# Set-up chains, an output bias on GpSimd and layer 3's first graph ahead of layer 2's tail, in a four-layer graph kernel

## The reference

```python
x = _layernorm(x + _L0_gnn_ref(x, ...))   # relational: sum_r (adj==r) @ ((xW + b_r) * sigmoid(xWWg + bg_r)), relu
x = _layernorm(x + _L1_gnn_ref(x, ...))   # bilinear attention with leaky relu, masked softmax, elu
x = _layernorm(x + _L2_gnn_ref(x, ...))   # 8-head attention, masked; out @ Wo.T + bo
x = _layernorm(x + _L3_gnn_ref(x, ...))   # 8-head additive attention, leaky relu, masked softmax
```

## Time and profile before

| | us |
|---|---|
| median of 3 runs | 737.16 |
| lowest, highest | 736.97, 738.91 |
| profiled execution | 739.22 |
| its span, first to last instruction | 737.5 |

### The profile page before, as it was taken

One profiled execution on the slowest core, in us unless ns is written; L12 is line 12 of the kernel. 1 busy time (PEld: TensorE's weight loads), 2 busy tenths in 40 slices (PEclk: granted clock), 3 DMA queues, 4 the chain that ended last, 5 costly groups with the idle time before them and its releaser, 6 DMA issues.

```text
span 737.5 us, 17528 instructions
## 1 busy us (share of the span) xinstructions
PE 661.7 (90%) x6402; PEld 496.5 (67%) x6402; DVE 604.1 (82%) x1534; ACT 541.3 (73%) x855; POOL 492.8 (67%) x522
## 2 busy tenths in 40 slices
PE   2999799999779999999999998789999999999982
PEld 1788578777446666666666666567777777777751
DVE  4699849999678888888888885789888888888882
ACT  1545379988458777777777776478898998989982
POOL 6377528999675466676566664347777667776685
PEclk9999799999689999999999999899999999999997
DMA  8900000000000000000000000000000000000001
GB/s 232 285 6 1 1 1 1 2 1 2 0 1 2 1 1 2 3 2 2 2 1 3 2 1 1 1 2 2 16 16 30 16 16 16 16 21 26 16 15 44
DMA packets 28885, 14.91 MB, mean 20 GB/s; under 512 B 1920, under 2 KB 28800, under 8 KB 28800
## 3 DMA queue, kind: packets, MB, share of 16 engines
q1 hardware_dynamic: 25344, 12.59, 6.1%
q10 hardware_dynamic: 3456, 1.20, 0.8%
HBM read 9.59 MB, written 4.19 MB: 19 GB/s over the span
## 4 chain that ended last, share of the span: by engine, by line
PE 45%; POOL 19%; DVE 14%; issue 11%; POOLq 7%; ACT 3%; DVEq 0%; ACTq 0%
PE pair L1036 15%; POOL arena L648 7%; POOLq L527 7%; POOL X L532 6%; PE pair L1220 5%; PE quad L1169 4%; DVE arena L1014 3%; DVE nmx L1020 3%; POOL yb L655 3%; PE quad L1084 2%; PE pair L1199 2%; PE pair L1185 2%; PE pair L1191 2%; PE pair L1156 2%; POOL ln L526 2%
## 5 line engine op out<-in xcount | busy, mean ns | idle before, releaser
L634 POOL TENSOR_TENSOR arena<-arena,nmx 128x1024 f32<-128x1024 f32 x64 | 121.3, 1895 | 91.5 <-DVE nmx L965 89.8
L648 POOL TENSOR_TENSOR arena<-arena,nmx 128x1024 f32<-128x1024 f32 x64 | 121.4, 1897 | 78.5 <-DVE nmx L1020 78.4
L1036 PE MATMUL pair<-identf,arena 128*128 128x128 f32 x1088 | 151.0, 281 | 0.9 <-DVE yb L988 0.9
L1036 PEld LDWEIGHTS pair<-identf,arena 128*128 128x128 f32 x1088 | 117.1, 141 | 31.5 <-issue 31.5
L532 POOL TENSOR_SCALAR X<-yb,ln 128x128 f32<-128x128 f32 x256 | 113.2, 454 | 9.0 <-issue 9.0
L526 POOL TENSOR_TENSOR ln<-ln,neghalf 128x4 f32<-128x4 f32 x64 | 66.6, 1041 | 33.0 <-DVE ln L566 32.9
L839 ACT ACTIVATE arena<-quad 128x1024 f32<-128x1024 f32 x64 | 66.0, 1032 | 24.1 <-PE quad L1120 24.0
L956 DVE TENSOR_TENSOR arena<-quad,mask 128x1024 f32<-128x1024 f32 x64 | 77.7, 1214 | 4.8 <-PE quad L1169 4.1
L965 DVE TENSOR_REDUCE nmx<-arena 128x8 f32<-128x1024 f32 x64 | 78.0, 1218 | 1.8
L1020 DVE TENSOR_REDUCE nmx<-arena 128x8 f32<-128x1024 f32 x64 | 78.0, 1218 | 1.7
L1014 DVE TENSOR_TENSOR arena<-quad,arena 128x1024 f32<-128x1024 f32 x64 | 77.7, 1215 | 0.0
(11 more groups left out here) (195 smaller groups left out, 1435.8 us busy)
## 6 DMA issues: line engine op xcount, KB each, us to landing
X<-in_x SPq DMA_DIRECT2D x16, 256.0 KB, 6.1
arena<-in_adj SPq DMA_DIRECT2D x16, 256.0 KB, 6.2
out<-X SPq DMA_DIRECT2D x16, 256.0 KB, 2.3
...
```

The lines of the kernel that those rows point to most:

```text
L634: nc.gpsimd.tensor_tensor(v3(P2[t % 3], HEADS), v3(P2[t % 3], HEADS), nmx2[t % 2][:].unsqueeze(2).broadcast_to([128, HEADS, N]), ALU.add)\
L648: nc.gpsimd.tensor_tensor(v3(p, HEADS), v3(p, HEADS), nmx2[(t - 1) % 2][:].unsqueeze(2).broadcast_to([128, HEADS, N]), ALU.add)\
L1036: last = nc.tensor.transpose(dst[:, cols(i)], src[:, cols(i)], identf[:])
```

## The change

- Set-up: ScalarE issues the two weights, then six DMAs of one row each straight to the partitions 0, 32 and 64 of `bias_rest`, and a dummy Sigmoid. It copies the first three preparations in place of VectorE, which clears `bias3` and splits the bias when the six rows are there; the last subtraction is gone, two copies become one, and the `vx` tiles are cleared afterwards. TensorE starts its preparations with the two weights. GpSimd makes the identity before the other tiles. The copies of the bias to 128 partitions become the last two of the other parameters.
- Layer 0: ScalarE's Relu comes before the `xT` copy. At batch 15 VectorE takes the largest relation behind its masks and makes the flag after `yb` of batch 14. TensorE transposes it, does 13 preparations (in the banks 1, 2, 6, 7) and reads the flag before its last product. The other preparations go into the general branch.
- The output bias is no longer split, and its product leaves `project_out`. GpSimd adds `bo2` to `X` at the third graph of each batch in layer 2, after that batch's transposes. The bias sum and layer 3's weights move into the second step of layer 1 (`late_weights`).
- Layer 3: ScalarE's scaled copy and VectorE's two maxima of graph 0 (`EARLY` = 1) stand at the start of `layer2(64)`.

The diff, cut to its core. Left out are the reordering of the preparation list, the new arguments of the general branches, the bodies of `leaky` and `row_max` (the old lines with t in place of t - 1), and the two additional parameter loads.

```diff
-LAP = 6
+LAP, EARLY = 6, 1
...
+bvo_at = add(bvo[:], qk_bias[:, 3:4].broadcast_to([128, 128]), oT_w[:], oT_at)
+add(wa1[:], w1T[:], a_cols[:, 0:1].broadcast_to([128, 128]), w1_at)
+usual = len(prep)
 gT_at = {k: add(gT[k][:], nat[f"L0_gnn_Wg_{k}"]) for k in ("fwd", "bwd")}
...
+def read_flag(eng):
     eng.wait_ge(sem("flag_set"), 1)
-    value = eng.value_load(flag[0:1, 0:1], min_val=0, max_val=1)
+    return eng.value_load(flag[0:1, 0:1], min_val=0, max_val=1)
+def if_general(eng, value, body):
...
+def masks_of_heads(dve):
...
+def late_weights(dve):
     dve.wait_ge(sem("prep"), bvo_at + 1)
     nc.vector.tensor_tensor(bo2[:], bvo[:], bo_row[:], ALU.add).then_inc(sem("bo_set"), 1)
-    for part in range(3):
-        at = slice(32 * part, 32 * part + 1)
-        dve.wait_ge(sem("bo_set"), 2 + 2 * part)
-        nc.vector.tensor_copy(bo_part[:], bo2[:]).then_inc(sem("bo_set"), 1)
-        dve.wait_ge(sem("bo_set"), 3 + 2 * part)
-        nc.vector.tensor_copy(v3(bo3[at, :], G), bo_part[at, :].unsqueeze(1).broadcast_to([1, G, D]))
-        nc.vector.tensor_tensor(bo2[:], bo2[:], bo_part[:], ALU.subtract).then_inc(sem("bo_set"), 1)
...
+    nc.gpsimd.memset(bias_rest[:], 0.0)
     nc.gpsimd.memset(minus_one[:], -1.0)
-    nc.gpsimd.memset(center[:], 0.0)
-    nc.gpsimd.memset(sel1[:], 0.0)
-    nc.gpsimd.memset(sel2[:], 0.0)
-    nc.gpsimd.memset(headmask[:], 1.0)
-    nc.gpsimd.memset(neghalf[:], -0.5).then_inc(sem("pool_set"), 1)
+    nc.gpsimd.memset(identf[:], 0.0).then_inc(sem("pool_set"), 1)
...
     select(identf[:], [[-1, 128]], 0)
+    nc.gpsimd.memset(ones[:], 1.0)
     nc.gpsimd.tensor_copy(identb[:], identf[:]).then_inc(sem("ident"), 1)
+    nc.gpsimd.memset(neghalf[:], -0.5)
+    for s in range(2):
+        nc.gpsimd.memset(v3(y2x[s][:], G)[:, :, D:D + 1], 1.0)
+    nc.gpsimd.memset(center[:], 0.0)
+    nc.gpsimd.memset(headmask[:], 1.0)
+    nc.gpsimd.memset(sel1[:], 0.0)
+    nc.gpsimd.memset(sel2[:], 0.0).then_inc(sem("pool_set"), 1)
+    steps += 1
+    pool.wait_ge(sem("pool_set"), steps)
...
+    def layer0(b, s, turn):
+        if b == BATCHES - 1:
+            value.append(read_flag(pool))
+        norm_pool(pool, 0, b, s, turn)
+    value = []
+    every_batch(pool, layer0)
+    general_pool(pool, value[0])
...
+        b, j = t // G, t % G
+        if j == 2 and real(b):
+            if b == 0:
+                pool.wait_ge(sem("bo_set"), 1)
+            pool.wait_ge(sem("L2_xT_mm"), b + 1)
+            x = v3(x_of(b), G)
+            nc.gpsimd.tensor_tensor(x, x, bo2[:].unsqueeze(1).broadcast_to([128, G, D]), ALU.add)\
+              .then_inc(sem("L2_x_bo"), 1)
...
+    act.dma_start(nat["L0_gnn_W_loop"], t["L0_gnn_W_loop"][:, :]).then_inc(sem("L0_params"), 16)
+    act.dma_start(nat["L0_gnn_Wg_loop"], t["L0_gnn_Wg_loop"][:, :]).then_inc(sem("L0_params"), 16)
+    act.wait_ge(sem("pool_set"), 1)
+    for part in range(3):
+        at = slice(32 * part, 32 * part + 1)
+        for half, n in enumerate(("b_loop", "bg_loop")):
+            act.dma_start(bias_rest[at, cols(half)], t[f"L0_gnn_{n}"][:, :]).then_inc(sem("bias_loaded"), 16)
+    nc.scalar.activation(act_warm[:], minus_one[:], ACT.Sigmoid)
...
-    act.wait_ge(sem("pool_set"), 1)
+    prep_copies(act, nc.scalar.copy, range(first))
     def layer0(b, s, turn):
+        if real(b):
+            act.wait_ge(sem(f"adj_loaded{b}"), 16)
+            need(act, sem("L0_top"), b - 1)
+            nc.scalar.activation(elu[s][:], adj_of(b), ACT.Relu, bias=minus_one[:],
+                                 accum_out=top[:, bass.ds(b, 1)]).then_inc(sem("L0_top"), 1)
         if real(b + 1):
             act.wait_ge(sem("L0_xT_mm"), b + 2)
             need(act, sem("L0_hg_mm"), b)
             nc.scalar.copy(xT[1 - s][:], bank[0]).then_inc(sem("L0_xT"), 1)
...
-            act.wait_ge(sem(f"adj_loaded{b}"), 16)
-            need(act, sem("L0_top"), b - 1)
-            nc.scalar.activation(elu[s][:], adj_of(b), ACT.Relu, bias=minus_one[:],
-                                 accum_out=top[:, bass.ds(b, 1)]).then_inc(sem("L0_top"), 1)
...
-    prep_copies(act, nc.scalar.copy, range(first, len(prep)))
-    general_act(act)
+    prep_copies(act, nc.scalar.copy, range(first, usual))
+    general_act(act, read_flag(act))
...
+    def slope(t):
+        if graph(t):
+            act.wait_ge(sem("L3_s_mm"), t + 1)
+            need(act, sem("L3_leaky"), t - 1)
+            nc.scalar.mul(t3[t % 2], pair[t % 2], ALPHA).then_inc(sem("L3_scaled"), 1)
     def layer2(t):
         b, j = t // G, t % G
+        if GRAPHS <= t < GRAPHS + EARLY:
+            slope(t - GRAPHS)
...
+        if t >= EARLY:
+            slope(t)
...
     nc.vector.memset(bias3[:], 0.0).then_inc(sem("dve_set"), 1)
...
-    prep_copies(dve, nc.vector.tensor_copy, range(first))
...
-    dve.wait_ge(sem("L0_params"), 64)
-    rest = hg_bias
+    dve.wait_ge(sem("bias_loaded"), 96)
     for part in range(3):
         row = slice(32 * part, 32 * part + 1)
-        nc.vector.tensor_copy(bias_part[:], rest[:]).then_inc(sem("bias_split"), 1)
+        nc.vector.tensor_copy(bias_part[:], bias_rest[:]).then_inc(sem("bias_split"), 1)
         dve.wait_ge(sem("bias_split"), 2 * part + 1)
-        for i in range(2):
-            nc.vector.tensor_copy(bias3[row, cols(i, 2 * D)], bias_part[row, :])
-        nc.vector.tensor_tensor(bias_rest[:], rest[:], bias_part[:], ALU.subtract).then_inc(sem("bias_split"), 1)
-        dve.wait_ge(sem("bias_split"), 2 * part + 2)
-        rest = bias_rest
+        last = nc.vector.tensor_copy(v3(bias3[row, :], 2), bias_part[row, :].unsqueeze(1).broadcast_to([1, 2, 2 * D]))
+        if part < 2:
+            last = nc.vector.tensor_tensor(bias_rest[:], bias_rest[:], bias_part[:], ALU.subtract)
+        last.then_inc(sem("bias_split"), 1)
+        if part < 2:
+            dve.wait_ge(sem("bias_split"), 2 * part + 2)
+    for s in range(2):
+        nc.vector.memset(vx[s][:], 0.0).then_inc(sem("dve_set"), 1)
...
+            if b == BATCHES - 1:
+                dve.wait_ge(sem("L0_top"), BATCHES)
+                nc.vector.tensor_reduce(topmost[:], top[:], AX.X, ALU.max).then_inc(sem("top_set"), 1)
...
+            if b == BATCHES - 1:
+                find_flag(dve)
             stats_dve(dve, 0, b - 1, 1 - s)
+        if b == BATCHES - 1:
+            dve.wait_ge(sem("L0_hg_mm"), BATCHES)
+            for i in range(2):
+                nc.vector.memset(xT[i][96:128, :], 1.0).then_inc(sem("ones_row"), 1)
...
-    find_flag(dve)
-    l3_weights(dve)
-    general_dve(dve)
+    general_dve(dve, read_flag(dve))
+    masks_of_heads(dve)
     def layer1(t):
+        if t == 1:
+            late_weights(dve)
...
+        if GRAPHS <= t < GRAPHS + EARLY:
+            leaky(t - GRAPHS)
+            row_max(t - GRAPHS)
...
             dve.wait_ge(sem("L2_o_mm"), b - 1)
+            dve.wait_ge(sem("L2_x_bo"), b - 1)
...
-        if graph(t - 1):
-            p = rows_of(t - 1)
...
-            need(dve, sem("L3_pT_mm"), t - 3)
-            nc.vector.tensor_tensor(p, pair[(t - 1) % 2], t3[(t - 1) % 2], ALU.max).then_inc(sem("L3_leaky"), 1)
+        if t > EARLY:
+            leaky(t - 1)
...
+        if t > EARLY:
+            row_max(t - 1)
...
     pe.wait_ge(sem("ident"), 1)
-    pe.wait_ge(sem("L0_params"), 64)
+    pe.wait_ge(sem("L0_params"), 32)
...
+        if b == BATCHES:
+            pe.wait_ge(sem("top_set"), 1)
+            nc.tensor.transpose(bank[0][0:1, 0:128], topmost[:], identf[:]).then_inc(sem("top_mm"), 1)
+            pe.wait_ge(sem("params"), sems["n_params"])
+            pe.wait_ge(sem("pool_ready"), 1)
+            prep_pe(pe, range(first, usual))
+            value.append(read_flag(pe))
...
+    value = []
     every_batch(pe, layer0, before=True, after=1)
-    pe.wait_ge(sem("params"), sems["n_params"])
-    pe.wait_ge(sem("pool_ready"), 1)
-    prep_pe(pe, range(first, len(prep)))
-    general_pe(pe)
+    general_pe(pe, value[0])
...
     def project_out(b):
         pe.wait_ge(sem("L2_onT"), b + 1)
-        if b == 0:
-            pe.wait_ge(sem("bo_set"), 8)
-        mm(out_bank(b), ones[:], bo3[:], start=True, stop=False)
         for g in range(G):
-            last = mm(out_bank(b)[:, cols(g)], onT[:, cols(g)], oT_w[:], start=False, stop=g == G - 1)
+            last = mm(out_bank(b)[:, cols(g)], onT[:, cols(g)], oT_w[:], start=True, stop=True)
```

116 lines of the change are left out of this document (51 added, 65 removed).

## The result

The changed kernel takes 721.19 us (median of 4 runs, 720.54 to 723.82); the kernel before, with the run on the same chip added, 737.83 us. The ratio is 0.977 (95% interval 0.975 to 0.979), 16.6 us less. The forecast was 723.8 in a range of 718.0 to 729.5, so the time lies inside the range and 2.6 us under the forecast. The two profiled executions differ by a little more, 739.2 and 720.5 us: their spans went from 737.5 to 718.7 us, 18.8 us, and this is the difference that the traces can be searched for.

The account below looks back on a forecast made before the run. No single engine bounds the whole; TensorE is busiest at 90%, and whichever engine arrives last decides each place. Terms 2.2 + 3.7 + 3.6 + 2.7 + 1.2 = 13.4 us gave a median of 723.8, range 718 to 729.5.

Parts of the forecast that it names:

- likeliest case: The forecast itself: all five terms pay and GpSimd's selections hold up the bias split; median 723.8 us, chance 0.50.
- Term A: Set-up: earlier first projection (0.7) and the Relu's new place (0.76) gain 2.2 us, between 1 and 7.3.
- the gate: Layer 0: VectorE's wait of 0.76 us for the gate of batch 2, taken away by the Relu's new place.
- TensorE's wait at 23.97: Layer 0: TensorE waited 0.70 us for the values of batch 0, which would come 2.1 us earlier.
- Rival 1: Set-up: the ports don't hold the bias split up; 4.9 us gained there, time 721.1; chance 0.17.
- the row at 207.07: Layer 1's end: VectorE operation begun 0.04 us before GpSimd's addition still lasted 1.96 us; held against the first-issuer rule.
- Term B: Layer 0 to layer 1: preparations and flag read ahead of the last product; layer 1 starts 3.7 us earlier (2.5 to 4.4).
- Term C: Layer 2's output bias: sixteen products leave TensorE, GpSimd's additions are covered; 3.6 us gained (0 to 3.7).
- Term D: Layer 2 to layer 3: early first graph removes TensorE and VectorE waits; 2.7 us, between 2.2 and 3.7, below: 0.
- Term E: Clock at the joins: TensorE could stay at the upper level; 1.2 us, bounds 1.0 at the first, 2.5 at the second.
- the slower rival: Layer 2: GpSimd's new addition lies on the path, 20.3 us come back, time 744.1; chance 0.04.

Follow-up runs that it names:

- sel_late: Changed kernel with one wait more: GpSimd starts its selections only when VectorE has split the bias; 717.99 us, ratio 0.974.

## Why the prediction was right, and where it was not

The forecast of 723.8 was 2.6 us too slow. Its likeliest case (all five terms pay, the ports hold the split up) is what happened, with terms A, B, D and E too small: 16.6 us came in place of 13.4.

**Term A: 2.2 forecast, 3.7 measured.** The mechanism was as told: the long operations of the split end where GpSimd's selections end. The step that failed is the landing of the one-row transfers. I took 5.0 us from the earlier trace rows, the row of the same size, and 4.1 for the last issue; it was issued at 3.48 and had landed by 7.35 in place of 9.1, inside my bounds (6.7 to 11.0). The split itself was near the forecast by two errors: 2.7 us of work under 3.5 us of stalls, where I had 3.2 under 2.7 (starting sooner, it met four selections and not three), so 6.2 in place of 5.9. That was luck. Together they give the projection at 13.65 instead of 15.0. The rest of the term, 0.76 + 0.70 for the gate and for TensorE's wait at 23.97, was forecast as 1.46 and came as 1.64. Rival 1 gave 721.1, almost the measured time, for a reason that is false: a case that lands on the number is not thereby the cause. What it described, a split without stalls, is sel_late, at 718.0.

Here the Trainium skill ("SBUF — State Buffer", section "Who interferes with whom") can be judged better than before the run. It says that whichever engine issues first has the shared ports for its whole instruction, and that a subtraction with both inputs in SBUF collides with a GpSimd instruction that reads SBUF. By the second rule the subtraction at 11.41 should stand still, and it took 1.35 us in place of 0.40. By the first, operations begun in a gap between two selections (7.35, 8.66) should go free, and they did. I had held the row at 207.07 against that rule, and wrongly: GpSimd's scaling ahead of that addition ran until 207.15, so the VectorE operation did not come into a gap. The chain did end at 13.5, the time that I had named for this rule, but from a start at 7.35 and not at 9.1, so the number bears nothing out. The same section has an operation with a single SBUF input and no fast mode go free, and the mask addition, which reads PSUM and one tile, kept its 1214 ns beside the doubled additions.

**Term B: 3.7 forecast, 4.3 measured** until layer 1's first transposes. The steps stand: 3.74 us of term A added, the first copy was at 77.90 (forecast 77.9) and the transposes at 82.8 (83.4). The failed step is small: a preparation is 0.23 us on the spot (13 from 74.16 to 77.12), not 0.25, and from the last copy's end to the product the flag read took 1.0 us (77.12 to 78.11), not 1.2. By the experiments 2.6 us of the term are the move of the 13 preparations and the flag read. The remaining 1.7 us agree with the seven preparations that are gone, 7 x 0.25, though no run took those alone. What was put behind the new wait is covered but for a rest: layer 0's last normalization and the moved weights end at 85.34 on VectorE, and of the 1.0 us that I had to spare nothing is left, since TensorE waits 0.43 us for the leaky maximum.

**Term C: 3.6 forecast, 3.66 measured**, a period shorter by 0.21 to 0.22, nothing lost to GpSimd. The cover was larger than I thought: behind the idle time of that one step, which I counted, a subtraction 0.46 us late still did no harm.

**Term D: 2.7 forecast, 3.1 measured** on the path, between the two ends (2.2 for TensorE's own waits, 3.7 for VectorE). At layer 3's third scores it is 2.4 us (they start 21.2 us behind the reciprocal of layer 2's graph 56 in place of 23.6), and 3.1 at the fourth, for which TensorE waits for VectorE. The 3.75 to 3.9 us between whole kernels with and without the early graph hold 0.6 to 0.8 us of clock besides, which the forecast had in term E.

**Term E: 1.2 forecast.** At the first join the step that failed is its bound. I allowed 1.0 there, since VectorE would be late next. It was late next, and its leaky maximum gained no more than 0.74 us on the transposes' start. But behind it TensorE had its projections of batch 0 in the queue, at half speed in the kernel before, and that made 2.4 us in the profiled pair. It is no fixed gain: the profiled runs without filler and with the same order of work had it in three cases of seven. At the second join the clock was low for some 7 us before and some 3 us after, 0.6 to 0.8 us in this pair, and it held in seven of the nine profiles with one early graph, where the gain is 2.3 us, near my bound of 2.5. The third join was left out: the prediction counts three joins at the lower clock and prices two. From layer 1's batch 8 to layer 2's graph 1 the kernel before took 72.7 us, the changed kernel 70.7, and this is the stretch with the 2.07 us that were not forecast. The ten profiled experiments with the same code there took anything from 70.7 to 72.9, so I take them for the clock too, and not for a steady gain.

**The sum.** The terms A to D come to 3.7 + 4.3 + 3.7 + 3.1 = 14.8 us, where the forecast had 12.2, and the medians differ by 16.6. Some 1.8 us are thus left for the clock in an ordinary run, where term E had 1.2; how they spread over the three joins no run shows. The range, which had been drawn over both states of the clock and both ends of the set-up, held the time for this reason. No steady stretch gave anything back, and the slower rival had no ground.
